# Layer two's node pass in a four-layer graph network: transposes one step ahead of the product

## The reference

```python
out = jax.ops.segment_sum(msg, dst, num_segments=n)
return jax.nn.elu(out.reshape(n, H * D))                  # end of L2
...
x = _layernorm(x + _L2_gnn_ref(x, src, dst, ...), axis=-1)
...
h = (x @ W.T).reshape(N, H, C)                            # start of L3
a_s = jnp.einsum('nhc,hc->nh', h, att_src)
a_d = jnp.einsum('nhc,hc->nh', h, att_dst)
```

## Time and profile before

| what | value |
|---|---|
| median of 3 executions | 5962.21 us (5940.05 to 5986.56) |
| the profiled execution | 5980.64 us |
| its span from first to last instruction | 5978.9 us |
| granted clock of PE over the span | 0.861 |
| PE, DVE, ACT, POOL busy | 72%, 62%, 33%, 60% of the span |
| mean transfer rate | 189 GB/s |

### The profile page before, as it was taken

How to read it: one execution, slowest core, us unless ns; L and a number is a source line. 1 busy time by engine, 2 the same in 40 slices (tenths; PEclk the granted TensorE clock), 3 DMA queues, 4 the chain that set the end, 5 groups by cost and what they waited for, 6 DMA issues and landing times. The chain is left out here.

```text
span 5978.9 us, 70346 instructions
## 1 busy us (share of the span) xinstructions
PE 4323.1 (72%) x16758; PEld 2871.5 (48%) x16758; DVE 3698.6 (62%) x10097; ACT 1977.5 (33%) x3345; POOL 3602.5 (60%) x3312
## 2 busy tenths in 40 slices
PE   7355569989999999999999777757766500016666
PEld 5233335556666666666666566645555400002222
DVE  6233255656665666666666466667767554558887
ACT  1011135532222222222222122237666300006666
POOL 4388744433556555555555566647666666658887
PEclk9677789999999999999999787779888755559998
DMA  9977789974433333333332333348878522229997
GB/s 371 290 137 139 125 278 366 366 290 140 141 119 118 118 116 119 120 117 118 121 118 90 102 120 120 122 158 309 285 271 283 193 81 84 85 96 344 352 349 289
DMA packets 499110, 1129.62 MB, mean 189 GB/s; under 512 B 165942, under 2 KB 248842, under 8 KB 498966
## 3 DMA queue, kind: packets, MB, share of 16 engines
q1 hardware_dynamic: 333466, 866.21, 41.5%
q0 software_dynamic: 113184, 174.84, 12.4%
q10 hardware_dynamic: 52316, 87.06, 4.1%
HBM read 627.40 MB, written 543.83 MB: 196 GB/s over the span
## 5 line engine op out<-in xcount | busy, mean ns | idle before, releaser
L1014 PE MATMUL psum<-W2b,arena 128*128 128x256 f32 x3136 | 727.0, 380 | 1.9 <-DVE arena L947 1.9
L991 PE MATMUL psum<-arena,W1b 128*128 128x512 f32 x1568 | 725.8, 606 | 0.0
L746 DVE TENSOR_SCALAR arena<-arena 128x256 f32<-128x256 f32 x784 | 462.5, 652 | 366.0 <-POOL arena L741 343.3
L1014 PEld LDWEIGHTS psum<-W2b,arena 128*128 128x128 f32 x3136 | 574.2, 191 | 69.3 <-issue 3.0
L1497 PE MATMUL psum<-Wg,arena 128*128 128x264 f32 x1568 | 436.6, 439 | 215.6 <-ACT arena L1523 123.0
L1700 PE MATMUL psum<-arena,ident 128*128 128x512 f32 x784 | 416.9, 682 | 203.3 <-POOL arena L1758 201.4
L904 ACT ACTIVATE arena<-psum,hbias 128x512 f32<-128x512 f32 x392 | 269.2, 687 | 857.3 <-PE psum L991 829.4
L1139 POOL DMA_INDIRECT tab<-arena,IDX x392 | 404.1, 1031 | 199.5 <-issue 118.9
L991 PEld LDWEIGHTS psum<-arena,W1b 128*128 128x128 f32 x1568 | 282.0, 190 | 430.9 <-issue 430.9
L1550 POOL DMA_INDIRECT ad_d<-arena,FE x392 | 401.9, 1025 | 129.8 <-issue 115.9
L737 POOL TENSOR_TENSOR arena<-arena,lneps 128x4 f32<-128x4 f32 x196 | 39.6, 202 | 730.3 <-DVE arena L733 729.8
(11 more groups left out here) (232 smaller groups left out, 9315.4 us busy)
## 6 DMA issues: line engine op xcount, KB each, us to landing
arena<-tab SPq DMA_DIRECT2D x194, 544.0 KB
arena<-x_d SPq DMA_DIRECT2D x202, 512.0 KB
arena<-in_x SPq DMA_DIRECT2D x194, 512.0 KB
x_d<-arena SPq DMA_DIRECT2D x194, 512.0 KB
tab<-zero SPq DMA_DIRECT2D x132, 486.0 KB
tab<-blank SPq DMA_DIRECT2D x97, 544.0 KB
h_d<-arena SPq DMA_DIRECT2D x97, 528.0 KB
arena<-h_d SPq DMA_DIRECT2D x97, 528.0 KB
```

Source lines behind the costliest of these rows:

```text
L746: v.tensor_scalar(y[:, j, :], r[:, j, :], self.mv[:, j, 0:1], self.rs[:, j:j + 1], ALU.subtract, ALU.mult).then_inc(self.s["y"], 1)
L991: last = pe.matmul(psum[:, BR + c % RING, :], W1b[:, f, c * P:(c + 1) * P], x1T[:, f, :], start=False, stop=(f == FH - 1))
L1014: last = pe.matmul(outB(j), hid[:, c, j * P:(j + 1) * P], W2b[:, c, :], start=(c == 0), stop=(c == KH - 1))
```

## The change

PE issues the transposes of step k+1 ahead of the product of step k. `xT` gets two buffers (2048 elements a partition instead of 1024 in the shared arena; the buffers behind it that are loaded early keep their place, since that is set by the end of the phase before). The product's counter `mm` now goes up twice a step, after the first two and after the last two of the four node groups, and DVE adds the bias in two halves of two groups each, so `hs` goes up twice as well; all waits for the two are scaled. ACT's copy waits for the product of two steps before instead of one.

```diff
-            xT = take([FH, STEP])
+            xT = take([2, FH, STEP])
...
-                    sp.wait_ge(r["hs"], k.s + 1)
+                    sp.wait_ge(r["hs"], 2 * (k.s + 1))
...
-                def body(k):
+                def tr(k):
                     pe.wait_ge(r["y"], J * (k.s + 1))
                     wait(pe, r["xT"], FH * k.s)
                     for f in range(FH):
                         for j in range(J):
                             last = pe.transpose(psum[:, f, j * P:(j + 1) * P], y[:, k.slot(NB), j, f * P:(f + 1) * P], ident[:, :])
                     last.then_inc(r["tr"], 1)
+
+                def body(k):
+                    if live(k.plus(1), NS):
+                        tr(k.plus(1))
                     pe.wait_ge(r["xT"], FH * (k.s + 1))
-                    wait(pe, r["hs"], k.s)
                     for j in range(J):
+                        if j % 2 == 0:
+                            wait(pe, r["hs"], 2 * (k.s - 1) + j // 2 + 1)
                         for f in range(FH):
-                            last = pe.matmul(psum[:, 2 + j, 0:HW], xT[:, f, j * P:(j + 1) * P], Wg[3][:, f, :], start=(f == 0), stop=(f == FH - 1))
-                    last.then_inc(r["mm"], 1)
+                            last = pe.matmul(psum[:, 2 + j, 0:HW], xT[:, k.slot(2), f, j * P:(j + 1) * P], Wg[3][:, f, :], start=(f == 0), stop=(f == FH - 1))
+                        if j % 2 == 1:
+                            last.then_inc(r["mm"], 1)
+                tr(beat(0, NB))
                 run_beats(pe, NS, body, NB)
...
-                    wait(act, r["mm"], k.s)
+                    wait(act, r["mm"], 2 * (k.s - 1))
                     for f in range(FH):
-                        act.activation(xT[:, f, :], psum[:, f, :], ACT.Copy).then_inc(r["xT"], 1)
+                        act.activation(xT[:, k.slot(2), f, :], psum[:, f, :], ACT.Copy).then_inc(r["xT"], 1)
...
-                    pool.wait_ge(r["hs"], k.s + 1)
+                    pool.wait_ge(r["hs"], 2 * (k.s + 1))
...
-                    v.wait_ge(r["mm"], k.s + 1)
                     out_wait(v, k)
                     wait(v, s_xd[b], 16 * J * k.turn(NB) + XD3[b])
-                    v.tensor_tensor(out=hs[:, b, :, :], in0=psum[:, 2:2 + J, 0:HW],
-                                    in1=bias3[:, :].rearrange("p (a d) -> p a d", a=1).to_broadcast([P, J, HW]), op=ALU.add).then_inc(r["hs"], 1)
+                    for i in range(2):
+                        v.wait_ge(r["mm"], 2 * k.s + i + 1)
+                        v.tensor_tensor(out=hs[:, b, 2 * i:2 * i + 2, :], in0=psum[:, 2 + 2 * i:4 + 2 * i, 0:HW],
+                                        in1=bias3[:, :].rearrange("p (a d) -> p a d", a=1).to_broadcast([P, 2, HW]), op=ALU.add).then_inc(r["hs"], 1)
```

## The result

The changed kernel takes 5906.3 us in the median of 4 executions (5889.9 to 5909.9), the kernel before 5956.6 us beside it (4 executions): ratio 0.9904, 95% interval [0.9877, 0.9931]. The medians differ by 50 us; the ratio, which is not that of the medians, stands for 57 us. The forecast of 5880 us was the right way and 26 us too low; the range of 5838 to 5942 holds it.

A forecast was written before the change was run, and what follows sets the result against it. A chain of waits through transposes, copy and product was taken to bound layer two's node pass; 6.4 + 0.3 = 6.7 us a step instead of 7.54 saves 82 us over 98 steps, 5962.2 to 5880 us, range 5838 to 5942.

The forecast's parts named there:

- The chain of transposes, copy and product: Layer two's node pass: the three run one after another, 5.88 us a step, PE idle 1.18 us for the copy.
- late releases: Node pass: ACT's copy and DVE's bias addition start about 2 us after PE's recorded end, part of 1.66 us a step.
- the first term: The node pass before the change: 739 us for 98 steps, 7.54 us a step, from which the gain was subtracted.
- The bias in halves: DVE's bias addition split in two: 0.1 us more a step, at most 0.15, with DVE still not the limit.
- the wait before the bias: Sign: DVE's idle time before the two halves stays over 50 us; over 150 us would prove the forecast wrong.
- POOL's wait for the variances: Sign: POOL's idle time in the node pass, 145.1 us before the change, falls under 60 us.
- the remaining disturbances: Late releases and slow-clock products left in the node pass: 0.3 of 1.66 us a step, bounds 0 and 0.75.
- The 6.4: Transfer bound of an undisturbed node-pass step: 2.13 MB at 333 GB/s give 6.4 us.
- POOL's 6.1 us a step: POOL's scatters, issue gaps and powers in the node pass: 600 us in all, close behind but not yet the limit.
- the main case of 5858 to 5905 us: The forecast case for the total, around 6.7 us a step and 5880 us; chance 0.50.
- The rival in which transfers or POOL hold the pass: They hold the node pass at about 7.15 us a step: gain 38 us, total 5924 us (5906 to 5940); chance 0.24.
- The rival of the clock: PE drops to 1.2 GHz for more of the node pass: 8.36 us a step, total 6042 us; chance 0.06.

The follow-up runs named there:

- condition A: Group of executions (another chip or another state of one) in which the kernel before takes 5957 to 5961 us beside the experiments.
- e1: Changed kernel with the bias in one piece again, only the transposes ahead with two buffers: pass 666.7 us, total 5915.8 us, ratio 0.9921 to the kernel before.
- e4: Changed kernel with the next step's transposes between the product's two halves instead of ahead of it: pass 737.4 us, total 5971.5 us, ratio 1.0021 to the kernel before.
- e7: Changed kernel with one POOL scatter a step instead of four (output wrong), condition B: pass 572.2 us, ratio 0.9915 to the kernel before.
- condition B: Group of executions (another chip or another state of one) in which the kernel before takes 5712 to 5717 us beside the experiments.
- e9: Changed kernel run again without edit, in condition B: pass 600.3 us, total 5702.9 us, ratio 0.9979 to the kernel before.
- e6: Kernel before with this pass's loads cut to a quarter of their bytes (output wrong), condition B: pass 610.9 us, ratio 0.9998 to the kernel before.
- e11: Kernel before with this pass's loads cut to a quarter of their bytes (output wrong), condition A: pass 724.3 us, ratio 1.0053 to the kernel before.
- e8: Kernel before with one POOL scatter a step instead of four (output wrong), condition B: pass 581.6 us, ratio 0.9943 to the kernel before.
- e5: Changed kernel with this pass's loads cut to a quarter of their bytes (output wrong), condition B: pass 601.1 us, ratio 0.9978 to the kernel before.

## Why the prediction came out as it did

The chain of transposes, copy and product, with the late releases in it, was the limit in condition A, and the change takes it out. The forecast for the pass was 657 us and 6.7 us a step; 654.4 and 6.68 were measured. PE's 1.18 us of idle time between transposes and product are gone. e1 shows that this part alone brings the gain; e4 shows that the place of the transposes decides, and its rows point to the wait for the bias.

The step that was off is the first term: 7.54 us a step for the pass before, read from one execution. Three executions give 7.54, 7.32 and 7.24. The middle one makes the pass gain 63 us, and with it 5962 - 63 = 5899 us, 7 us from the measured 5906 (13 us from the 5956.6 that the kernel before took beside it). I had noted that the profiled execution lay 18 us over its median, and subtracted a gain from the median that was worked out from the slow execution alone; this pass alone was 21 us longer in it than in the middle one. The rest is elsewhere: of the 74 us between the two profiled spans (5978.9 and 5904.5) the pass gives 84, and other phases took 10 back without being touched.

The bias in halves was priced at 0.1 us of DVE a step; 130.9 against 123.0 us over 98 steps is 0.08. A half took 702 ns where 671 to 690 was taken. As forecast the wait before the bias stays over 50 us (90.8) and the DMA share is about 0.9 (0.89); the rate of 310 GB/s and the clock of 0.93 only just reach the values that they were to exceed. The copy's wait fell to 47.6 us instead of under 40, POOL's wait for the variances to 68.5 instead of under 60.

That the remaining disturbances come to 0.3 us a step came out right in sum: 6.68 less 6.4. The 6.4 in it was not a limit: it was 2.13 MB at the rate of a stretch with a DMA share of 0.97, but that stretch didn't show the most that the queue gives: in e7 the rate was 367 GB/s over 400 us. In condition B the same kernel runs at 6.13, which is POOL's 6.1 us a step, worked out from the earlier trace rows. So the undisturbed step is 6.1 us and the disturbances in A are 0.55 us a step, inside the stated bounds of 0 and 0.75. That the two errors cancelled is luck.

The measured 5906.3 us also lies a hair outside the main case of 5858 to 5905 us, and the gain of over 1%, given 0.62, didn't come: it is 0.96% by the ratio, 0.84% by the medians. The band in which it falls was meant for the case that transfers or POOL hold the pass at 7.15 us a step; the pass at 6.68 says that it is the main case after all.

The rival in which transfers or POOL hold the pass is true in condition B for POOL, and there for both orders (6.13 us a step in e9, 6.23 in e6), which is why the change gives 0.2% there instead of 1.0%. Its supposed cause, that transfers delay the releases, e11 speaks against as far as loads go, and e9 for full queues. The rival of the clock came to nothing: the idle time of a step fell and the clock rose. The Trainium skill (TensorE: Matmul & The Clock Gate, Part 4: PE-mode transpose) would have transposes count less for the clock. Between 4000 and 4400 us the two orders show nearly the same clock at the same load: 1.00 in e7 and e8, 0.96 in e5 and 0.97 in e6. So these runs speak neither for that rule nor against it.

Open stays what makes the releases late in condition A. It isn't the volume of the loads (e11), and full queues come without late releases in B (e9). The number of indirect stores and the bytes of the stores weren't tried in A.

## What to carry to other kernels

Where an engine's result is copied by another engine for the engine's own next step, put the making of it ahead of that step's work: it is then early and absorbs delays that you can't remove (e1). Look also at which waits it stands behind: e4 lost the whole gain with the transposes behind a wait for the bias that the copier doesn't share. Splitting a consumer in halves without that order brought nothing here. Before you price a chain of waits, profile the kernel more than once: this pass differed by 29 us between three executions of one kernel, half of what the change gained, and a change that removes stalls is worth only as much as there are stalls where it runs. And don't take a full DMA share for a limit before a run with fewer bytes has shown it.

## What the runs showed of the hardware

Signals of PE can come late and bundled in one condition (the two increments of `mm` at 4195.57 and 4195.66 us for half products that end 1.8 us apart) and on time in the other, in the same program: in e9 the trace has no wait without a named releaser at all. The longest of condition A stand at the end of the pass, here in the changed kernel:

```profile
4637.43 1.04 PE L1491 MATMUL psum<-ident,arena 128*128 128x128 f32 x8
...
4640.60 2.05 PE L1502 MATMUL psum<-Wg,arena 128*128 128x264 f32 x8 [0.35 <-DVE arena L1576]
...
4645.52 1.08 ACT L1530 ACTIVATE arena<-psum 128x512 f32<-128x512 f32 x2 [9.76 <-remote]
...
4652.71 1.32 DVE L1576 TENSOR_TENSOR arena<-psum,bias 128x528 f32<-128x528 f32 x2 [12.16 <-remote]
```

The copy, which waits for PE's counters alone, starts 7 us after the recorded end of its transposes (4638.47). The two halves of the bias start from 4652.71, 10 us after the recorded end of the second half product (4642.65); by the trace's record of the counters `mm` goes up at 4652.59 and 4652.68, once for each half. Not every increment of the counters is in the record in condition A (80 of the 98 of `tr` here; in e9 all are there). Up to 4600 us no wait of this kind is above 6.2 us, and most are between 0.4 and 3.

What condition A costs is 54 us in this pass for the changed kernel (654.4 against 600.3). For the kernel before it is about 106, if e6 stands for it in B as e5 does for e9 (717.4 against 610.9).
